# A recurrence and local-attention kernel on one NeuronCore: the first tile of each layer, the first up-projection, the recurrence gates and the split of w1 in other places

## The chip, the core and the metric

The kernel runs on one core of a Trainium2 chip. The core has a matrix engine (TensorE, PE), three elementwise engines (VectorE or DVE, ScalarE or ACT, GpSimd or POOL) and a sync engine (SP) that issues the DMAs. Each engine takes its own instructions strictly in the written order, and they wait for each other through semaphores. The metric is the device time of one execution in microseconds (us).

## What is computed

The input x is 16 sequences of 512 rows with 128 features. After a layer norm (xn) two branches use it, and the output is x + s * silu(f).

```python
def _layernorm(x): m = mean(x, -1); v = var(x, -1); return (x - m) / sqrt(v + 1e-05)

def recurrence(x):                      # s
    x_conv = causal_depthwise_conv(x, conv_w, conv_b)          # width 4
    r_t = sigmoid(x_conv @ W_r.T + b_r); i_t = sigmoid(x_conv @ W_i.T + b_i)
    a_t = sigmoid(log_a) ** (8.0 * r_t)
    h_t = a_t * h_(t-1) + sqrt(clip(1.0 - a_t * a_t, 0.0)) * i_t * x_conv
    out = h @ W_out.T
    return out * rsqrt(mean(out * out) + 1e-06) * gamma

def layer(x):                           # f, applied twice (DEPTH = 2)
    h = shift_token(x)                  # half of the features come from the row before
    q, k, v = split(h @ wqkv)           # 8 heads of 64
    q, k = l2norm(q) * q_scale, l2norm(k) * k_scale
    q, k = rotary_xpos(q, k)
    o = softmax(8 * q @ k.T + mask) @ v # windows of 64 rows, looking at this one and the last
    x = x + o @ wo
    h = layernorm(shift_token(x)) * lg + lb
    a, g = split(h @ w1 + b1)           # 128 -> 2 x 341
    return x + (a * gelu(g)) @ w2 + b2
```

## The kernel before

Everything stays in SBUF: X holds the 16 sequences transposed (features on the partitions), A the copy for the recurrence, B the normalised activations. A sequence has four tiles of 128 rows, so a layer has NT = 64 tiles and NB = 16 sequences. The order on every engine is written out by hand: each engine's function runs the same loops, and what stands in an iteration is chosen by the iteration number.

**Attention of a layer** is `for i in range(NT + 4)`. In iteration i, PE makes q and k of tile i (`qk_proj`, six matmuls into banks 0 and 1), turns q and k of tile i-2 (`turn_qk`, L234 and L237), works out its scores (`sims`), turns the softmax of tile i-3 (`turn_p`, L224), applies tile i-4 to the values (`attend`) and makes v of tile i (`v_proj`). ACT squares q and k (`square`, L530), takes the root (`norm_rt`), the exponentials (`exps`, L556) and copies (`keep_q`, `keep_v`, `keep_p`, `keep_o`). DVE applies the rotary tables (`rotate`, L802 and L793), sums the squares (`norm_sum`, L809), copies k (`keep_k`, L840 and L841) and finds the row maximum (`row_max`, L821). POOL adds (`add_qk`) and scales (`scale_qk`) q and k and normalises the softmax, all through L1040. `qk_proj` of a tile waits until `rotate` has read the tile before it, since both use banks 0 and 1.

Between these stand the other steps, one sequence in four iterations: in layer 0 the input layer norm of a sequence (`ln_stats` on DVE, `ln_root` on ACT, `ln_apply` on POOL L1067, `ln_turn` on PE L172, `ln_keep` on ACT L474, then a DMA that shifts a half into hsh, then `shift_hi` L1076 and `shift_lo` L1040 on POOL, which split it into the two parts hT that the matmuls use); in layer 1 the recurrence (`rec_decay`, `rec_a2`, `rec_root` L725, `rec_root2`, `rec_input`, `rec_scan`, `rec_out`, `rec_gamma`); in both the projection with wo and the second layer norm (`mean`, `centre`, `square_hc`, `var`, `log_var`, `root_var`, `scale_hc`).

**The last four iterations of attention** (i = 64 to 67) drain it. In iteration 66 w1 is scaled and split into w1r (ACT L685, DVE L999) and the first sequence into hnr; at the end of 67 PE makes the bias from w1 (`bias1`).

**The up and down loop** is `for b in range(NB + 3)`: `up(b)` is 18 matmuls with w1r (three chunks j, each a gate part into bank 3+j and an input part into bank j), ACT applies gelu (L603), DVE multiplies (`hidden`, L903), `down` is six matmuls, `down_add` (L909) adds to X. In layer 0 the gates of the recurrence are made here: `conv` on DVE (L725, L918), `gates` and `gates2` on PE and tanh on ACT (L608, L614). `gates(b-1)` and `gates2(b-1)` stand in iteration b, so sequence 15's come in iteration 16, next to `qk_proj(1, 0)`, the first tile of layer 1. Iterations 1 and 2 also finish the layer norm of sequence 15, for which ACT loads the table set with Ln and Exp. In layer 1 the loop holds `end_turn`, `rec_scale`, `end_out` and the stores.

SBUF space is shared in time: w1r and hnr of the up and down loop lie over t1, t2, t3 and sqk of attention, and hxf over P, PT, qT and a part of kT.

## Time and profile before

| | before |
|---|---|
| median of 3 runs | 1361.43 us (1360.09 to 1361.75) |
| the profiled execution: its own time | 1365.7 us |
| its span, first to last instruction | 1363.9 us |
| mean granted TensorE clock | 0.987 |
| busy: PE, DVE, ACT, POOL | 1273.0, 1112.1, 1109.0, 1019.8 us |

From the trace, the stages are: the start until about 46 us; attention of layer 0 until 556.8; its up and down loop until about 699; attention of layer 1 until 1236.9; its up and down loop and the output until the end. Busy PE time counts matmuls whose ends are modelled, and a matmul at the lower clock level counts for twice as long. So a stage is read by three things together: PE's busy time, its granted clock, and what its idle time waited for.

### The profile page before, as it was taken

The page shows a single profiled execution, that of the slowest core. Times are in us where ns is not written, and L with a number is a line of the kernel's source. Part 1 is how long each engine was busy: PE and PEld are TensorE (multiplying, and loading weights), DVE is VectorE, ACT ScalarE, POOL GpSimd, SP SyncE. Part 2 cuts the span into 40 slices and gives each one's busy share as a digit, 9 for nine tenths or more (in the row PEclk, how much of TensorE's full clock was granted, in tenths as well). Part 3 has the DMA queues.
Part 4 walks back from the last instruction along what each step waited for, and adds up shares of the span by engine and source line. Part 5 has one row for each costly group of instructions (what it writes and reads, how often), then busy time and mean ns, then how long its engine had stood idle before and what let it go on. Part 6 is the DMA issues. An engine that isn't in the chain of part 4 may idle for free.

```text
span 1363.9 us, 37604 instructions
## 1 busy us (share of the span) xinstructions
PE 1273.0 (93%) x13656; PEld 994.9 (73%) x13656; DVE 1112.1 (82%) x1929; ACT 1109.0 (81%) x3418; POOL 1019.8 (75%) x712
## 2 busy tenths in 40 slices
PE   2799999999999999899978999999999999999997
PEld 1687887878788787555547788888878888876664
DVE  3788888888888886578768898999889999873887
ACT  2689999999998998564448999999999999997664
POOL 4799999999999987212138999999999999972110
PEclk9899999999999999999989999999999999999999
DMA  5222222222222211011011212211122112110222
GB/s 154 51 60 60 67 60 60 67 60 60 60 73 65 65 41 33 16 32 29 0 26 33 47 45 47 50 44 44 46 55 48 44 44 48 37 32 25 77 72 83
DMA packets 60599, 70.33 MB, mean 52 GB/s; under 512 B 8960, under 2 KB 38528, under 8 KB 60416
## 3 DMA queue, kind: packets, MB, share of 16 engines
q1 hardware_dynamic: 60416, 67.93, 20.0%
q8 instruction: 110, 1.80, 0.6%
q14 instruction: 73, 0.60, 0.1%
HBM read 13.40 MB, written 4.19 MB: 13 GB/s over the span
## 4 chain that ended last, share of the span: by engine, by line
PE 85%; ACT 5%; issue 4%; DVE 3%; POOL 1%; SPq 1%; DMA 1%; ACTq 0%; DVEq 0%
PE ps L167 68%; PE ps L224 9%; PE ps L234 4%; PE ps L237 4%; ACT P L556 2%; DVE t L793 1%; POOL side L1067 0%; PE ps L172 0%; DMA B<-in_k_scale 0%; PE ps L377 0%; ACT qT L577 0%; DVE nm L821 0%; DVE t L802 0%; ACT sqk L530 0%; ACT Vn L570 0%
## 5 line engine op out<-in xcount | busy, mean ns | idle before, releaser
L556 ACT ACTIVATE P<-ps,nm 128x128 f32<-128x128 f32 x1024 | 364.4, 385 | 5.2 <-DVE nm L821 5.2
L167 PE MATMUL ps<-wqkv,hT 128*128 128x512 f32 x1152 | 332.2, 432 | 28.0 <-DVE t L793 12.3
L1040 POOL TENSOR_TENSOR P<-P,rden 128x512 f32<-128x512 f32 x256 | 293.0, 1151 | 42.8 <-DVE rden L828 40.7
L1040 POOL TENSOR_TENSOR t<-t 128x1024 f32<-128x1024 f32 x128 | 306.5, 2395 | 19.1 <-DVE t L793 17.3
L167 PEld LDWEIGHTS ps<-wqkv,hT 128*128 128x128 f32 x1152 | 218.4, 192 | 106.1 <-issue 39.4
L1040 POOL TENSOR_TENSOR t<-t,rr 128x1024 f32<-128x1024 f32 x128 | 243.6, 1903 | 26.1 <-ACT rr L539 25.9
L556 ACT ACTIVATION_READ_ACCUMULATOR P<-ps,nm 128x1 f32 x1024 | 231.1, 226 | 0.0
L802 DVE TENSOR_TENSOR t<-ps,tabl 128x512 f32<-128x512 f32 x256 | 164.2, 683 | 48.1 <-ACT sqk L530 46.9
L546 ACT ACTIVATE PT<-ps 128x1024 f32<-128x1024 f32 x128 | 130.6, 1020 | 75.0 <-PE ps L224 74.0
L1040 POOL TENSOR_TENSOR hnr<-B,hnr 128x512 fp32r<-128x512 f32 x32 | 41.2, 1287 | 198.7 <-ACT hnr L594 198.7
L821 DVE TENSOR_REDUCE nm<-ps 128x4 f32<-128x512 f32 x256 | 173.8, 680 | 6.8 <-PE ps L167 6.8
L793 DVE TENSOR_TENSOR t<-ps,tabl 128x1024 f32<-128x1024 f32 x128 | 155.3, 1213 | 0.0
L809 DVE TENSOR_REDUCE sums<-sqk 128x16 f32<-128x1024 f32 x128 | 154.6, 1208 | 0.0
L530 ACT ACTIVATE sqk<-ps 128x1024 f32<-128x1024 f32 x128 | 137.9, 1077 | 13.7 <-PE ps L167 9.8
L167 PE MATMUL ps<-hnr,w1r 128*128 128x512 f32 (+1 forms) x576 | 146.2, 407 | 0.5 <-DVE hxf L903 0.3
L224 PE MATMUL ps<-idf,P 128*128 128x128 f32 x1024 | 142.2, 281 | 2.1 <-POOL P L1040 2.0
L841 DVE COPY kT<-ps 128x512 f32<-128x512 f32 x128 | 87.9, 686 | 62.7 <-PE ps L237 62.4
L167 PE MATMUL ps<-kT,qT 64*64 64x128 f32 x4096 | 136.3, 271 | 0.0
L167 PE MATMUL ps<-PT,Vs 128*64 128x64 f32 x2048 | 133.2, 229 | 0.4 <-ACT Vn L570 0.2
L167 PEld LDWEIGHTS ps<-kT,qT 64*64 64x64 f32 x4096 | 123.7, 134 | 8.4 <-issue 0.3
L224 PEld LDWEIGHTS ps<-idf,P 128*128 128x128 f32 x1024 | 109.1, 140 | 26.8 <-issue 22.9
L167 PEld LDWEIGHTS ps<-hnr,w1r 128*128 128x128 f32 (+1 forms) x576 | 100.2, 176 | 37.0 <-issue 7.6
(120 smaller groups left out, 2445.6 us busy)
## 6 DMA issues: line engine op xcount, KB each, us to landing
Vs<-Vn SPq DMA_DIRECT2D x224, 128.0 KB, 2.3
side<-in_x SPq DMA_DIRECT2D x16, 256.0 KB, 3.2
hsh<-X SPq DMA_DIRECT2D x32, 128.0 KB, 2.3
A<-X SPq DMA_DIRECT2D x16, 256.0 KB, 2.5
h<-X SPq DMA_DIRECT2D x32, 128.0 KB, 2.3
oT<-in_x SPq DMA_DIRECT2D x16, 256.0 KB, 3.0
out<-oT SPq DMA_DIRECT2D x16, 256.0 KB, 2.4
hsh<-X SPq DMA_DIRECT2D x32, 127.8 KB, 2.3
```

The costliest lines, as they stand in the source:

```text
L167: return e.matmul(o, lhsT, rhs, start=start, stop=stop, skip_group_check=True)
L224: k = e.transpose(ps[:, 5 + g // 4, (g % 4) * 128:(g % 4 + 1) * 128], P[:, g, :], idf[:])
L234: k = e.transpose(ps[:, 5, c * 128:(c + 1) * 128], c0[:, c * 128:(c + 1) * 128], idf[:])
L530: act(heads(sqk[:]), ps[:, 0:2, :].rearrange("p i (h e) -> p (i h) e", e=DH), ACT.Square).then_inc(s_sq, 1)
L546: act(PT[:], ps[:, 5:7, :].rearrange("p s (g q) -> p (s g) q", g=4), ACT.Copy).then_inc(s_PT, 1)
L556: k = act(P[:, g, :], ps[:, 3 + s, (g % 4) * 128:(g % 4 + 1) * 128], ACT.Exp, bias=nm[:, g:g + 1], accum_out=den[:, g:g + 1])
L793: e.tensor_tensor(o1, qk, C, ALU.mult).then_inc(s_t2, 1)
L802: e.tensor_tensor(o2[:, :, :, 32 * s:32 * s + 32], qk[:, :, :, 32 - 32 * s:64 - 32 * s], S[:, :, 32 * s:32 * s + 32].unsqueeze(2).to_broad ...
L809: e.tensor_reduce(sums[:, :, 0], heads(sqk[:]), AX, ALU.add).then_inc(s_ss0, 1)
L821: e.tensor_reduce(nm[:, 4 * s:4 * s + 4], S4, AX, ALU.max, negate=True).then_inc(s_nm, 1)
L841: e.tensor_copy(kT[:, :, s0:s0 + 128], ps[:, 6, :].rearrange("p (c q) -> p c q", c=4)).then_inc(s_kt, 1)
L1040: return e.tensor_tensor(o, a, b_, op)
```

## The change

It has six parts.

1. **The first tile of a layer a cycle ahead.** `turn_qk`, `sims`, `keep_q`, `keep_k` and `row_max` of tile 0 move from iteration 2 to iteration 1, and `norm_rt` of tile 0 from iteration 1 to 0. In layer 1, `rotate` and `norm_sum` of tile 0 and its `qk_proj` and `square` move into iteration b = 15 of layer 0's up and down loop. The zeroing of kT and Vs becomes `no_tile`: in layer 0 the first thing on POOL, in layer 1 in iteration 1, with `rec_a2(0)` and `rec_a2(1)` behind it.
2. **The first up-projection in the drain of attention.** `up(0)` is taken apart into `up_in` and `up_gate`: two input parts ahead of `turn_p` in iteration 66, two gate parts behind it, the third gate part in iteration 67, the third input part in the loop.
3. **w1 at home.** w1r has space of its own, w1 is loaded into the space of sq and rsd, and `bias1` and the two steps of the split move to iterations 2, 3 and 4 of a layer. The space of t1 and t2 is no longer shared with the up and down loop (`kept`).
4. **Gates shifted by a sequence.** `gates(b)` and `gates2(b)` stand in iteration b, and `conv(b + 1)` one iteration ahead of `hidden(b + 1)`; `conv(0)` is in the drain.
5. **The input layer norm's last step** on POOL is x * rst + nmr in place of (x - mean) * rst, with nmr = -mean * rst made by two more instructions per sequence, and `ln_apply(1)` stands behind the first `shift_hi` and `shift_lo`. wqkv's third part is split ahead of the tables.
6. **Smaller ones.** One preloaded table set in iteration 2 of the loop where Ln and Exp each brought a load; one `rec_rms` in place of two; `rec_root` as a tensor_tensor with min; `set_decay` in iterations 9 to 11.

The diff, cut:

```diff
+            sp_("kept", [128, 2048])
             hnr = sp_("hnr", [128, 2, 2, L], F32R)
...
+            def up_gate(l, b, j):
+                m, (o, n) = l * NB + b, CH[j]
+                if b:
+                    e.wait_ge(s_gl, 3 * (m - 1) + j + 1)
+                elif j < 2:
+                    e.wait_ge(s_e, 2 * (l + 1) * NT - 1 + j)
+                else:
+                    e.wait_ge(s_PT, (l + 1) * NT)
+                three(l, b, 3 + j, HID + o, n).then_inc(s_ug, 1)
+
+            def up_in(l, b, j):
+                m, (o, n) = l * NB + b, CH[j]
+                if b:
+                    e.wait_ge(s_hxf, 3 * (m - 1) + j + 1)
+                elif j == 0:
+                    e.wait_ge(s_wlo, 4 * (l + 1))
+                    e.wait_ge(s_hnlo, m + 1)
+                    e.wait_ge(s_t2, (l + 1) * NT)
+                elif j == 2:
+                    e.wait_ge(s_xadd, 2 * (l + 1) * NB)
+                three(l, b, j, o, n).then_inc(s_ua, 1)
...
-                    if 0 <= i - 2 < NT:
+                    if 0 < i - 2 < NT:
                         turn_qk(l, i - 2)
...
+                    if i == NT + 2:
+                        up_in(l, 0, 0)
+                        up_in(l, 0, 1)
                     if 0 <= i - 3 < NT:
                         turn_p(l, i - 3)
+                    if i == NT + 2:
+                        up_gate(l, 0, 0)
+                        up_gate(l, 0, 1)
+                    if i == NT + 3:
+                        up_gate(l, 0, 2)
+                    if i == 2:
+                        bias1(l)
...
+                        turn_qk(l, 0)
+                        sims(l, 0)
                 for b in range(NB + 3):
-                    if b < NB:
+                    if 0 < b < NB:
                         up(l, b)
-                    if l == 0 and b == NB:
-                        e.wait_ge(s_hxf, 3 * NB)
+                    if l == 0 and b < NB:
+                        gates(b)
+                    if b == 0:
+                        up_in(l, 0, 2)
+                    if l == 0 and b == NB - 1:
+                        e.wait_ge(s_hxf, 3 * NB - 1)
                         qk_proj(1, 0)
...
+                    if i == 0:
+                        norm_rt(l, 0)
...
+                    if i == 1:
+                        keep_q(l, 0)
+                    if i == 3:
...
+                        act(w1r[:, 0, :], w1, ACT.Copy, scale=lcol(l, 0)).then_inc(s_whi, 1)
+                    if i == NT + 1:
+                        e.wait_ge(s_tpk, (l + 1) * NT)
+                        split_hn(l, 0)
...
                     if b == 2:
+                        e.preload_act_table_set(ATTN)
                         log_var(l, NB - 1, 7)
                         root_var(l, NB - 1)
-                        if l:
-                            rec_rms(1)
...
+                        if l == 0 and b == NB - 1:
+                            for p in range(3):
+                                rotate(1, 0, p)
+                            norm_sum(1, 0)
+                        if l == 0 and b + 1 < NB:
+                            conv(b + 1)
...
                 e.wait_ge(s_ln, b + 1)
+                tt(nmr[:], mv[:, :, 0], rst[:], ALU.mult).then_inc(s_nmr, 1)
+                e.wait_ge(s_nmr, 2 * b + 1)
+                e.tensor_scalar(nmr[:], nmr[:], -1.0, None, ALU.mult).then_inc(s_nmr, 1)
+                e.wait_ge(s_nmr, 2 * b + 2)
                 if b:
                     e.wait_ge(s_tx, b)
                 for t in range(TPB):
-                    k = e.tensor_scalar(xnb[:, t * 128:(t + 1) * 128], xb[:, t, :], mv[:, t, 0:1], rst[:, t:t + 1],
-                                        ALU.subtract, ALU.mult)
+                    k = e.tensor_scalar(xnb[:, t * 128:(t + 1) * 128], xb[:, t, :], rst[:, t:t + 1], nmr[:, t:t + 1],
+                                        ALU.mult, ALU.add)
...
-            ln_apply(0)
-            ln_apply(1)
...
             for l in range(DEPTH):
                 if l == 0:
+                    no_tile()
+                    ln_apply(0)
                     shift_hi(0, 0)
                     shift_lo(0, 0)
+                    ln_apply(1)
```

On POOL, at the very start, this stood before (layer norm of sequences 0 and 1, the zeroing, then hT of sequence 0):

```order
L1067 TENSOR_SCALAR side<-side,mv,rst 128x128 [waits s_ln]
L1067 TENSOR_SCALAR side<-side,mv,rst 128x128 x3
L1067 TENSOR_SCALAR side<-side,mv,rst 128x128 [waits s_tx,s_ln]
L1067 TENSOR_SCALAR side<-side,mv,rst 128x128 x3
L1107 MEMSET kT 128x4x64
L1108 MEMSET Vs 64x512
L1076 TENSOR_SCALAR hT<-hsh 128x512 [waits s_hsh]
L1040 TENSOR_TENSOR hT<-hsh,hT 128x512 [waits s_hi]
```

And this stands there now:

```order
L1138 MEMSET kT 128x4x64
L1139 MEMSET Vs 64x512
L1070 ISA
L1070 TENSOR_TENSOR nmr<-mv,rst 128x4 [waits s_ln]
L1096 TENSOR_SCALAR nmr<-nmr 128x4 [waits s_nmr]
L1101 TENSOR_SCALAR side<-side,rst,nmr 128x128 [waits s_nmr]
L1101 TENSOR_SCALAR side<-side,rst,nmr 128x128 x3
L1110 TENSOR_SCALAR hT<-hsh 128x512 [waits s_hsh]
L1070 TENSOR_TENSOR hT<-hsh,hT 128x512 [waits s_hi]
L1070 TENSOR_TENSOR nmr<-mv,rst 128x4 [waits s_ln]
```

The split of sequence 0 has moved ahead of the norm of sequence 1, and each norm has two small new instructions in front.

On PE, in iterations 66 and 67 of layer 0, the softmax of tile 63 is turned (L224), and then, before, everything else of the drain, the bias (cols,w) and `up(0)` (hnr,w1r) follow:

```order
L224 MATMUL ps<-idf,P 128x128 [waits s_pn,s_kt,s_qk]
L224 MATMUL ps<-idf,P 128x128 x3
L224 MATMUL ps<-idf,P 128x128 [waits s_pn]
L224 MATMUL ps<-idf,P 128x128 x3
L167 MATMUL ps<-rsd,avg 128x512 [waits s_sqh,s_xadd]
L167 MATMUL ps<-PT,Vs 64x64 [waits s_vlo3,s_o,s_vhi3,s_PT]
...
L167 MATMUL ps<-oT,wo 128x256 [waits s_o,s_rv]
L167 MATMUL ps<-oT,wo 128x256 x3
L167 MATMUL ps<-cols,w 128x1 [waits s_t2,s_w1]
...
L167 MATMUL ps<-hnr,w1r 128x512 [waits s_e,s_hnlo,s_wlo]
```

Now, at the same place (side,wr is `gates`):

```order
L172 MATMUL ps<-hnr,w1r 128x512 [waits s_t2,s_hnlo,s_wlo]
L172 MATMUL ps<-hnr,w1r 128x512 x5
L231 MATMUL ps<-idf,P 128x128 [waits s_pn,s_kt,s_qk]
...
L172 MATMUL ps<-hnr,w1r 128x512 [waits s_e]
L172 MATMUL ps<-hnr,w1r 128x512 x2
L172 MATMUL ps<-norm,avg 128x512 [waits s_sqh,s_xadd]
L172 MATMUL ps<-PT,Vs 64x64 [waits s_vlo3,s_o,s_vhi3,s_PT]
...
L172 MATMUL ps<-hnr,w1r 85x512 [waits s_PT]
L172 MATMUL ps<-hnr,w1r 85x512 x2
L172 MATMUL ps<-oT,wo 128x256 [waits s_o,s_rv]
```

Fifteen of the 18 matmuls of `up(0)` have moved to places ahead of the last projection (oT,wo), and the bias is gone from here.

On DVE, at the passage from layer 0 to layer 1, stood before (from the last `hidden`'s iteration on: L909 is `down_add`, L922 `gates2`, L725 with s_a2 `rec_root`):

```order
L909 SCALAR_TENSOR_TENSOR X<-ps,cols,X 128x512 [waits s_y]
L922 SCALAR_TENSOR_TENSOR A<-oT 128x512 [waits s_ti]
L802 TENSOR_TENSOR t<-ps,tabl 128x16x32 [waits s_add,s_tabm,s_sq,s_ua]
L802 TENSOR_TENSOR t<-ps,tabl 128x16x32
L793 TENSOR_TENSOR t<-ps,tabl 128x1024 [waits s_tpk]
L909 SCALAR_TENSOR_TENSOR X<-ps,cols,X 128x512 [waits s_y]
L922 SCALAR_TENSOR_TENSOR A<-oT,side 128x512 [waits s_ti]
L725 TENSOR_SCALAR side<-side 128x512 [waits s_a2]
L809 TENSOR_REDUCE sums<-sqk 128x16 [waits s_sq]
L813 TENSOR_REDUCE ss<-sums 128x16 [waits s_rr0,s_ss0]
L802 TENSOR_TENSOR t<-ps,tabl 128x16x32 [waits s_add,s_sq]
```

And now:

```order
L826 TENSOR_TENSOR t<-ps,tabl 128x16x32 [waits s_tabm,s_add,s_sq]
L826 TENSOR_TENSOR t<-ps,tabl 128x16x32
L817 TENSOR_TENSOR t<-ps,tabl 128x1024 [waits s_tpk]
L833 TENSOR_REDUCE sums<-sqk 128x16 [waits s_sq]
L837 TENSOR_REDUCE ss<-sums 128x16 [waits s_rr0,s_ss0]
L933 SCALAR_TENSOR_TENSOR X<-ps,cols,X 128x512 [waits s_y]
L946 SCALAR_TENSOR_TENSOR A<-oT 128x512 [waits s_ti]
L933 SCALAR_TENSOR_TENSOR X<-ps,cols,X 128x512 [waits s_y]
L865 COPY kT<-ps 128x4x128 [waits s_sim,s_zero,s_tpk]
L826 TENSOR_TENSOR t<-ps,tabl 128x16x32 [waits s_add,s_sq]
```

The rotation and the sums of tile 0 have moved ahead of both of the last two `down_add`, `rec_root` has gone behind tile 1, and the copy of k of tile 0 has come ahead of the rotation of tile 1.

## Rows read from the trace of the kernel before

**Rows 1.** Page: share of the chain that ended last, by engine.

```profile
PE 85%; ACT 5%; issue 4%; DVE 3%; POOL 1%; SPq 1%; DMA 1%; ACTq 0%; DVEq 0%
```

**Rows 2.** Stretches: span, busy PE, PEld, DVE, ACT, POOL, granted clock, DMA.

```profile
68.00:102.00 34.00, 32.98 (x411) 27.67 (x410) 29.39 (x57) 29.80 (x103) 32.64 (x24) 1.00 0.24 60
...
602.00:636.00 34.00, 34.00 (x114) 20.32 (x113) 27.88 (x42) 15.99 (x26) 5.17 (x4) 1.00 0.20 54
```

**Rows 3.** Stretches of 2 us, same columns: drain of layer 0, start of layer 1.

```profile
548.00:550.00 2.00, 1.32 (x9) 0.86 (x8) 0.00 (x0) 0.93 (x3) 1.04 (x1) 0.97 0.00 0
550.00:552.00 2.00, 2.00 (x18) 0.87 (x18) 0.00 (x0) 2.00 (x4) 0.53 (x1) 0.50 0.03 8
...
706.00:708.00 2.00, 0.00 (x0) 0.00 (x0) 1.84 (x3) 0.03 (x1) 1.42 (x2) 0.72 0.00 0
708.00:710.00 2.00, 0.00 (x0) 0.00 (x0) 0.98 (x2) 1.97 (x4) 0.42 (x1) 0.50 0.01 4
```

**Rows 4.** Timeline of the start: start us, us, engine, line, operation, idle before it.

```profile
0.24 0.10 POOL L1337 MEMSET const-float32-0.0<- 128x1 f32 x1 [0.24 <-issue]
...
10.61 0.60 ACT L474 ACTIVATE X<-ps 128x512 f32<-128x512 f32 x1 [3.38 <-PE ps L172]
...
15.11 3.12 POOL L1067 TENSOR_SCALAR side<-side,mv,rst 128x128 f32<-128x128 f32 x4 [5.76 <-ACT rst L470]
...
18.91 0.61 POOL L1076 TENSOR_SCALAR hT<-hsh 128x512 fp32r<-128x512 f32 x1
...
21.01 2.90 PE L167 MATMUL ps<-wqkv,hT 128*128 128x512 f32 x6 [10.44 <-POOL hT L1040]
...
26.51 0.60 SPq L1167 DMA_DIRECT2D hsh<-X  x1
...
28.07 4.41 PE L167 MATMUL ps<-wqkv,hT 128*128 128x512 f32 x12 [3.51 <-DVE wqkv L772]
...
35.35 2.92 PE L167 MATMUL ps<-wqkv,hT 128*128 128x512 f32 x6 [2.87 <-DVE t L793]
```

**Rows 5.** Waits between 100 and 500 us: total us, times, longest.

```profile
PEld ps L234 <- POOL t L1040: 2.4, 12, 0.2
```

**Rows 6.** POOL's and DVE's lines in a steady stretch of layer 0, and L1067 in all.

```profile
311.81 1.29 DVE L840 COPY kT<-kT 128x256 f32<-128x256 f32 x1 [0.75 <-PE ps L237]
...
L1067 POOL TENSOR_SCALAR side<-side,mv,rst x64: 787/795/1397, 5.6 to 466.3; 128x128 f32<-128x128 f32 x64
```

**Rows 7.** Timeline of the drain of layer 0 and the first iterations of its loop.

```profile
549.10 0.66 PE L224 MATMUL ps<-idf,P 128*128 128x128 f32 x4 [0.68 <-POOL P L1040]
...
553.89 1.96 PE L167 MATMUL ps<-oT,wo 128*128 128x256 f32 x8 [0.79 <-ACT oT L586]
555.70 1.25 PE L167 MATMUL ps<-cols,w 128*128 128x1 f32 x12
...
557.29 1.28 ACT L603 ACT_TABLE_LOAD   x1 [2.50 <-DVE b1g L872]
...
571.95 4.77 PE L167 MATMUL ps<-hnr,w1r 128*128 128x512 f32 x18
...
591.34 1.12 PE L167 MATMUL ps<-oT,wr 128*128 128x512 f32 x2 [0.78 <-ACT B L608]
```

**Rows 8.** Timeline from the last down-projection of layer 0 into layer 1.

```profile
697.14 1.02 ACT L530 ACTIVATE sqk<-ps 128x1024 f32<-128x1024 f32 x1
...
703.96 2.56 DVE L725 TENSOR_SCALAR side<-side 128x512 f32<-128x512 f32 x1 [2.04 <-POOL side L1040]
...
711.50 2.93 PE L167 MATMUL ps<-wqkv,hT 128*128 128x512 f32 x6 [6.49 <-DVE t L793]
...
721.22 1.67 PE L167 MATMUL ps<-wqkv,hT 128*128 128x512 f32 x6 [0.42 <-DVE t L793]
```

**Rows 9.** Timeline of the end of the drain of layer 1.

```profile
1229.79 0.66 PE L224 MATMUL ps<-idf,P 128*128 128x128 f32 x4 [0.17 <-POOL P L1040]
...
1236.90 3.30 PE L167 MATMUL ps<-hnr,w1r 128*128 128x512 f32 x13
```

224 lines of the change are left out of this document (102 added, 122 removed).

## The prediction

> **What bounds the kernel now.** I read first the chain that ended last: 85% of the span is PE's [rows 1]. Then the stretches: in attention PE is busy for 32.98 of 34 us and POOL for 32.64, in the up and down loop PE for 34.00 of 34, all at the full clock level (granted 1.00, 2.4 GHz) [rows 2]. So in the long middle of each stage no reordering of other engines' work can give much, and the time to be had lies at the seams: the start, the two drains of attention, the passage from layer 0 to layer 1. There PE idles, and behind the idling the granted clock falls to 0.50, the 1.2 GHz level: in the drain of layer 0 PE was busy for 1.32 of 2 us when the clock began to fall, and in the passage it fell while PE had nothing to do at all [rows 3]. Last I read, in the timelines, which wait ends last at each seam.
>
> **Part by part.** The sums are made against the span of 1363.9 us. The profiled execution took 1365.7 us, 4.3 above the median of 1361.43; what I subtract from the span I subtract from the median.
>
> *The start.* Before, hT of sequence 0 was ready for splitting from about 14.2 us (the copy to X ended at 11.2, and the DMA needs about 3 us with its issue), but the split stood behind `ln_apply(1)`, 3.12 us from 15.11 on, and began at 18.91. The first `qk_proj` began at 21.01; the second stood behind `v_proj(0)`, which waited 3.51 us for the third part of wqkv, and the third began at 35.35 [rows 4]. The new order takes both waits away: the split at about 12.5 (if `ln_apply(0)` is done some 2 us earlier; 14.5 if not), `qk_proj(0)` 2.1 us later at 14.6, 6.4 ahead of 21.01. But most of this is given back. `turn_qk(0)` now stands ahead of `qk_proj(2)`, and it needs `scale_qk(0)`, which on POOL stands behind the split of sequence 1. That needs `ln_keep(1)` on ACT, which now waits behind `norm_rt(0)`: square and rotation and sum of tile 0 (1.0 + 2.4 + 1.4 us after the 2.9 of `qk_proj`) end at 22.3, so the copy ends at 23.5 against 25.98, its second DMA is issued near 24.1 against 26.51 [rows 4], and split and scaling (1.9 + 1.9 us after a landing of 2.3) give `turn_qk(0)` at 30.4. Turning at the low clock takes 1.7, then DVE copies k (0.7), does the statistics of sequence 2 (1.3) and the rotation (2.4): `qk_proj(2)` at 36.6, later than 35.35. Tile 0's scores are then already done, so the next cycle is shorter: `qk_proj(3)` at about 43.3 against 45.06. I take **1.7 us**, and 1.3 more because the third `ln_apply`, which in this cycle stands alone in front of `scale_qk(2)`, is shorter: **3.0**. Bounds: -2 (the split at 14.5 and a dearer norm) and 6.4 (nothing given back).
>
> *The norm on POOL, 16 times.* Four instructions over 128x128 took 795 ns each in the median; `shift_hi`, a multiply and an add with constants over four times as many columns, took 0.61 in one [rows 4, 6]. The new form is the same pair of operations, with two columns as operands, for which the trace has no row. Lower bound 0.15 (a quarter of 0.61), upper bound the longest of the old form, 1.40 [rows 6]. I take 0.25, since the nearest row in operations is `shift_hi`. The two 128x4 instructions have no row either; I take 0.55 with their two waits, between 0.2 (twice the 0.10 of the memset of one column that opens the trace [rows 4]) and 1.6 (two at the old form's 0.79). That makes 4 x 0.25 + 0.55 = 1.55 for 3.12. What of it reaches PE: in the steady stretch `turn_qk` waited for POOL 12 times in 400 us, 2.4 us in all, once per sequence [rows 5], so 0.2 x 15 = **3.0**. Another piece may come where DVE's kT copy (1.29 us for 128x256 [rows 6]) ran until POOL's instruction beside it ended; I count nothing for it, and 7 as the upper bound, 0.5 a sequence. If the form is no cheaper, 4 x 0.79 + 0.55 = 3.7 is 0.55 more per sequence, and 8 are lost in place of 3 gained.
>
> The Trainium skill ("GPSIMD Engine Reference", section "Engine selection") says that on GpSimd one-input work runs at roughly line rate and two-input work at half. The old form, one input and 795 ns for 128 columns, does not agree with that; `shift_hi`'s row does. By that rule the new form would cost about what I take, and the sum would stay.
>
> *The drain of layer 0.* From the end of `attend(62)` (546.7) PE waits twice for POOL's softmax (1.1 and 0.68), for the copy (then 8 us of which 3.4 at half clock), and 0.79 for oT; then the bias, 1.25, and `up(0)` from 556.81 [rows 7]. A part j is three matmuls, 0.8 us (4.77 / 18 x 3). Laid out anew at the full clock: two input parts to 548.3, `turn_p(63)` to 549.7 (its second half is still bound by 549.10), two gate parts to 551.2, `var` to 551.7, `attend(63)` to 552.8, the third gate part to 553.6, the projection to 555.2. Then ACT is late next: root, split and a table load of 1.28 us, three gelus and tanh end at 558.7, and `gates2(0)`, which stands ahead of `up(1)`, waits for it. `up(1)` from 559.6, `gates(1)`, `down(0)`, `gates2(1)`, `mean`, and `up(2)` at 569.9 against 571.95 [rows 7]: **2.0 us**, with one sequence's gates more behind it, which counts in the passage. Bounds 0 and 5.3 (the 4.0 of the 15 moved matmuls and the 1.25 of the bias).
>
> *Iteration 2 of the loops.* One table load of 1.28 us fewer in layer 0, two in layer 1. In layer 0 PE waited 0.78 us for ACT behind them [rows 7], in layer 1 less. **0.8** together; 0 to 2.
>
> *The passage.* Let T be the end of `up(15)`, 689.8. Before, `gates(15)`, `down(15)`, `gates2(15)` followed `qk_proj(1,0)`; its square was at 697.14, `rec_root(0)` held DVE for 2.56 us in front of the sums, and `qk_proj(1,2)` began at 711.50 = T + 21.7, `qk_proj(1,3)` at 721.22 = T + 31.4 [rows 8]. Now: gates (0.9), `qk_proj(1,0)` (1.6), `down(14)` (2.6), `gates2(15)` (0.9) to T + 5.9; DVE rotates and sums to T + 7.5 and only then does `down_add(14)`, for which `down(15)` waits until T + 8.2: a new wait of 2.3 us on PE. `v_proj(0)`, `qk_proj(1)`, `v_proj(1)` to T + 14.0, `turn_qk(0)` to 14.9, the copy of k to 15.7, and only behind it the rotation of tile 1 to 18.2: `qk_proj(1,2)` there, 3.5 ahead. Square 1.0, sums, two `rec_root` at 0.7 (from a tensor_tensor of 0.68), rotation 2.4: `qk_proj(1,3)` at T + 24.6, 6.8 ahead. POOL then binds one cycle and takes 0.8 back: 6.0. PE still idles for 2.3, 1.2 and 2.7 us of these 25, and before, less idling than that brought the clock down in the drain [rows 3], so I take off 1.5 for some work at the low level: **4.5**. Bounds 1 (the low level through the whole fill) and 7.
>
> *The drain of layer 1.* The same layout with less idling: `turn_p(63)`'s second half at 1229.79, `up(0)` at 1236.90 [rows 9]. New: PE is full from 1229.0 to the projection's end at 1237.1, ACT then needs root, `rec_rms`, split, load and gelu to 1239.2, and `up(1)` starts there against 1241.6 (1236.9 + 4.77): **2.4**; 0 to 5.
>
> *What is moved elsewhere.* Bias (1.25 on PE), scaling of w1 (0.85 on ACT), its rest (1.35 on DVE) now stand in iterations 2 to 4 of each layer. There PE waits for other engines, so the bias hides; the 1.35 on DVE may lengthen a cycle by half: **-0.7** each, **-1.4** in all. w1's second load stands behind `shift_h` and a wait for s_hn on SP's queue; only `load_w2(1)` is behind it, which waits anyway until the end of the loop. `conv(b+1)` comes no earlier before its use than `conv(b)` did; `set_decay` is 2 us of tiny steps under PE. The later `rec_root` at 0.68 for 0.53 hides. Zero for all of them.
>
> Sum: 3.0 + 3.0 + 2.0 + 0.8 + 4.5 + 2.4 - 1.4 = 14.3. Span 1349.6; time 1361.4 - 14.3 = 1347.1, say **1347**.
>
> **Rivals.** (a) *The new form of the norm is not cheaper on POOL.* Against it speaks `shift_hi`; for it, that no row has columns as operands at that price. Then the steady term is -8 for +3, and the start about 0 for 3: 14.3 - 11 - 3 = 0.3 to 3 better at the full price, about 5 if half the price comes through: 1356 to 1361, taken as 1357. (b) *The seams stay bound by their chains.* The new waits named above (`ln_keep(1)` behind `norm_rt(0)`, `down_add(14)` behind the rotation, the copy of k ahead of tile 1's rotation) and the low clock level eat the gain, each term at its lower third: about 6 better, 1355. (c) *Slower.* The four-instruction norm at its dearest row, 1.40 us each, costs 4 x 1.40 + 0.55 = 6.15 per sequence, 3 more than now, right in front of `scale_qk`, for which PE already waits there; 15 x 3 = 45 less a slack of about 1 each, 30, minus the 8 of the seams: 1383. It decides from 0.75 us per sequence on, where 15 x 0.75 equals the 11.3 that the other terms give, that is at 0.83 us per instruction (3.12 + 0.75 - 0.55, over 4), hardly above the old 0.795. (d) *The steady stretch of layer 0 gives the kT copies too*: 7 more, 1340.
>
> The Trainium skill ("SBUF — State Buffer", section "Who interferes with whom") says that a VectorE copy in a two-port mode and a GpSimd instruction exclude each other for their whole length, whoever comes first. The 1.29 us copy agrees with it; by that rule a shorter norm shifts which instruction the copy meets, and does not take the meeting away, which is why (d) is not the forecast.
>
> **How the numbers follow.** Forecast 0.56 (1342 to 1352), (a) 0.14, (b) 0.14, (c) 0.07, (d) 0.09. A measurement of this kernel can tell about 0.2%, 2.7 us, from no change: 1358.7 to 1364.1. A third of (a) and a fifth of (b) fall in it: same 0.08; slower is (c) with a little of (a): 0.08; faster 0.84. The range leaves out (c) and the ends of (a), (b) and (d): 1340 to 1358.
>
> **What would show it.** Right: `qk_proj(0,0)` near 14.6 and `qk_proj(0,3)` near 43; the norm's line on POOL at about 0.25 us and no wait of `turn_qk` for POOL per sequence; 15 matmuls of `up(0)` ahead of the last projection and `up(2)` of layer 0 about 2 us earlier relative to `attend(62)`; `down(15)` waiting some 2 us for `down_add(14)`; `qk_proj(1,3)` 25 to 27 us after `up(15)`. Wrong: POOL's norm instructions above 0.8 us, a longer interval between equal tiles in attention of layer 0, or a clock of 0.50 for as long as before at the passage.

## The result and the profile after

| | before | changed |
|---|---|---|
| median | 1361.34 us (1360.09 to 1361.75, 4 runs) | 1353.37 us (1352.94 to 1354.10, 4 runs) |
| the profiled execution: its own time, its span | 1365.7, 1363.9 us | 1352.9, 1351.1 us |
| ratio, 95% interval | | 0.9944 (0.9926 to 0.9961) |

The change makes the kernel 8.0 us faster by the medians of this set, which is 0.6%. In a later set of runs the kernel before came out at 1367.69 us and the changed one at 1353.60: ratio 0.9899 (0.9885 to 0.9912), 14.1 us. The changed kernel repeats, the kernel before does not (1361.3, 1365.7, 1367.7 and 1363.3 us in four sets).

Where the time went is read best from one event that occurs once per tile in both kernels: the start of `turn_qk` on PE. Between its starts at chosen tiles, and from the last of them to `down`, lie the stages. Each kernel was profiled twice, and the measured gain is given over all pairings of the two profiles.

| stage (us) | before, twice | changed, twice | forecast gain | measured |
|---|---|---|---|---|
| start to tile 8 of layer 0 | 103.84, 103.48 | 101.95, 102.00 | 2.3 | 1.5 to 1.9 |
| tile 8 to 12 | 32.40, 31.47 | 35.92, 35.97 | 0 | -3.5 to -4.5 |
| tile 12 to 63 | 402.12, 402.10 | 397.18, 397.18 | 3.0 | 4.9 |
| tile 63 to down(1) | 39.06, 39.19 | 37.34, 37.33 | 2.0 | 1.7 to 1.9 |
| down(1) to tile 4 of layer 1 | 169.45, 168.37 | 164.21, 163.84 | 4.5 and part of 0.8 | 4.2 to 5.6 |
| tile 4 to 63 | 473.15, 472.00 | 473.50, 473.62 | -0.7 | -0.3 to -1.6 |
| tile 63 to down(3) | 50.25, 51.22 | 47.39, 47.56 | 2.4 and part of 0.8 | 2.7 to 3.8 |
| down(3) to the end | 93.63, 93.67 | 93.61, 93.70 | 0 | 0 |

The chain that ended last, by engine, has hardly changed (page of the changed kernel; compare [rows 1]), and the long middle of the loop is as full as it was (stretch, columns as in [rows 2]). In the drain of layer 0 the granted clock no longer falls (compare [rows 3]). In the passage it still does, but for two spells of 3.4 us each (from 692.2 and from 709.3), where it had stood at 0.50 for 13.7 us (from 706.9):

```profile
PE 83%; ACT 5%; issue 4%; DVE 3%; DMA 2%; POOL 2%; SPq 1%; ACTq 0%; DVEq 0%; POOLq 0%
```

```profile
602.00:636.00 34.00, 34.00 (x114) 20.30 (x113) 27.16 (x42) 15.41 (x24) 7.58 (x6) 1.00 0.17 46
...
548.00:550.00 2.00, 2.00 (x25) 1.15 (x25) 0.00 (x0) 0.76 (x2) 0.00 (x0) 1.00 0.00 0
550.00:552.00 2.00, 2.00 (x26) 1.43 (x21) 0.00 (x0) 1.60 (x4) 0.00 (x0) 1.00 0.00 0
692.00:694.00 2.00, 2.00 (x4) 0.87 (x3) 0.40 (x1) 1.30 (x2) 1.97 (x1) 0.56 0.00 0
```

The start, timeline of the changed kernel (compare [rows 4]): the first `qk_proj` comes at 15.99 us, where it had come at 21.01. Then `turn_qk(0)` waits until 31.67 for the scaling, which stood behind the split of sequence 1, and the third `qk_proj` comes at 37.92, later than the 35.35 of before:

```profile
15.99 2.90 PE L172 MATMUL ps<-wqkv,hT 128*128 128x512 f32 x6 [5.93 <-POOL hT L1070]
...
24.24 0.58 ACT L500 ACTIVATE X<-ps 128x512 f32<-128x512 f32 x1
...
27.79 0.62 POOL L1110 TENSOR_SCALAR hT<-hsh 128x512 fp32r<-128x512 f32 x1 [2.93 <-DMA hsh<-X]
28.49 1.26 POOL L1070 TENSOR_TENSOR hT<-hsh,hT 128x512 fp32r<-128x512 f32 x1
29.71 1.90 POOL L1070 TENSOR_TENSOR t<-t,rr 128x1024 f32<-128x1024 f32 x1
31.67 1.12 PE L241 MATMUL ps<-idf,t 128*128 128x128 f32 x4 [4.67 <-POOL t L1070]
...
37.92 2.93 PE L172 MATMUL ps<-wqkv,hT 128*128 128x512 f32 x6 [1.10 <-DVE t L817]
```

In this stretch the granted clock stands at 0.50 for some 22 us (from 24 to 46), where before it stood there from 28 to 30 and from 36 to 44.

The norm's line on POOL, and the carried copy of kT on DVE (L840 before, L864 now) between 140 and 520 us, first of the changed kernel, then of the kernel before (compare [rows 6]; columns of the groups: total us, mean ns, idle before it). One instruction of the norm takes 452 ns in place of 795, and with it the copy became shorter, 976 ns in the mean for 1585, though it was not changed:

```profile
L1101 POOL TENSOR_SCALAR side<-side,rst,nmr x64: 447/452/1424, 6.1 to 464.0; 128x128 f32<-128x128 f32 x64
...
L864 DVE COPY kT<-kT 128x256 f32<-128x256 f32 x12 | 11.7, 976 | 9.1 <-PE ps L244 9.1
```

```profile
L840 DVE COPY kT<-kT 128x256 f32<-128x256 f32 x12 | 19.0, 1585 | 9.0 <-PE ps L237 9.0
```

The wait of [rows 5], `turn_qk` for POOL, 12 times, is gone from the changed kernel's list for 137 to 535 us but for one. In the same list PE's idle time that ended in no wait the profile shows ("issue") fell with the copy, and PE now waits for a DMA three times (first of the changed kernel, then of the kernel before):

```profile
PE ps L172 <- issue: 4.3, 6, 0.8
...
PE ps L172 <- DMA norm<-X: 1.7, 3, 0.7
```

```profile
PE ps L167 <- issue: 10.1, 12, 1.5
```

New ahead of that stretch, in tile 8's cycle, is ScalarE's wait for the constants of the decay (`set_decay`). Timeline of the changed kernel:

```profile
100.68 2.38 POOL L1070 TENSOR_TENSOR t<-t 128x1024 f32<-128x1024 f32 x1
...
101.90 0.15 DVE L752 TENSOR_SCALAR ab<-ab 128x1 f32<-128x1 f32 x1
...
101.97 1.10 DVE L760 TENSOR_TENSOR ab<-cols,ab 128x1 f32<-128x1 f32 x1
...
103.11 0.20 ACT L712 ACTIVATE ab<-ab 128x1 f32<-128x1 f32 x1 [2.35 <-DVE ab L760]
```

The passage (compare [rows 8]; `gates(15)` begins at 683.45) and the drain of layer 1 (compare [rows 9]):

```profile
691.48 4.54 PE L172 MATMUL ps<-hxf,w 128*128 128x512 f32 x6 [2.19 <-DVE X L933]
...
702.79 1.66 PE L172 MATMUL ps<-wqkv,hT 128*128 128x512 f32 x6 [1.00 <-DVE t L817]
...
708.87 2.58 PE L172 MATMUL ps<-wqkv,hT 128*128 128x512 f32 x6 [2.51 <-DVE t L817]
```

```profile
1225.60 1.97 PE L172 MATMUL ps<-oT,wo 128*128 128x256 f32 x8
1228.09 0.91 PE L172 MATMUL ps<-hnr,w1r 128*85 128x512 f32 x3 [0.52 <-DVE X L873]
```

The drain of layer 0 has a new wait too. `conv(0)`, which part 4 of the change put there, holds VectorE for 3.5 us in front of the copy of k of tile 63, and the scores of tile 63 wait 1.77 us for that copy. They start 3.94 us behind `turn_qk(63)`; before, they waited 1.02 us for ScalarE and started 3.19 us behind it. First the changed kernel, then the one before:

```profile
534.04 1.23 DVE L749 TENSOR_SCALAR side<-A,cols 128x512 f32<-128x512 f32 x1
535.31 2.32 DVE L942 SCALAR_TENSOR_TENSOR side<-A,cols,side 128x511 f32<-128x511 f32 x3
...
538.21 0.69 DVE L865 COPY kT<-ps 128x512 f32<-128x512 f32 x1
...
538.99 0.41 PE L172 MATMUL ps<-mask,idb 64*64 64x512 bf16 x4 [1.77 <-DVE kT L865]
```

```profile
541.55 0.41 PE L167 MATMUL ps<-mask,idb 64*64 64x512 bf16 x4 [1.02 <-ACT qT L577]
```

### The profile page after: what moved, and what is told of

Its sections match the earlier page's. It is cut to its first block, busy times and chain, and to the rows that moved or that the text cites. A ratio compares the mean times of both kernels' runs of the same rounds, so it can differ in the third digit from the quotient of the medians.

```text
span 1351.1 us, 37630 instructions
## 1 busy us (share of the span) xinstructions
PE 1274.2 (94%) x13656; PEld 996.8 (74%) x13656; DVE 1104.1 (82%) x1929; ACT 1105.8 (82%) x3413; POOL 1009.0 (75%) x744
## 4 chain that ended last, share of the span: by engine, by line
PE 83%; ACT 5%; issue 4%; DVE 3%; DMA 2%; POOL 2%; SPq 1%; ACTq 0%; DVEq 0%; POOLq 0%
PE ps L172 66%; PE ps L231 9%; PE ps L241 4%; PE ps L244 4%; ACT P L580 2%; DMA norm<-X 1%; DVE t L817 1%; POOL t L1070 1%; DVE t L826 1%; ACT Vn L594 0%; PE ps L391 0%; PE ps L177 0%; DMA hsh<-X 0%; DVE sums L833 0%; POOL side L1101 0%
## 5 line engine op out<-in xcount | busy, mean ns | idle before, releaser
L1070 POOL TENSOR_TENSOR P<-P,rden 128x512 f32<-128x512 f32 x256 | 296.9, 1166 | 48.4 <-DVE rden L852 45.9
L1070 POOL TENSOR_TENSOR t<-t,rr 128x1024 f32<-128x1024 f32 x128 | 243.8, 1905 | 16.6 <-ACT rr L563 16.5
```

The lines of the kernel that those rows point to most:

```text
L1070: return e.tensor_tensor(o, a, b_, op)
```

## The experiments

Ratios are to the kernel before, which ran beside each set: at 1365.66 us in the first (decay_spread, old_norm, new_norm_before, start_order), 1367.69 in the second (after_again, copy_psum, drain_back, best1), 1363.31 in the third (decay_in_before, before_again, bias_weight, best2). The changed kernel itself ran in the second set only; a difference to it from another set leans on its two medians, 1353.37 and 1353.60. "Tiles 12 to 63" means the interval of `turn_qk` in layer 0.

One profile of a stage carries scatter. Kernels whose code is the changed kernel's up to the drain of layer 0 reached tile 8 at 101.95 and 102.00 (the changed kernel, twice), 103.01 (bias_weight) and 103.50 us (drain_back), and took 397.2, 397.2, 394.5 and 399.0 us from tile 12 to 63. So a difference of 1.5 us at the start, or of 2 to 4 us between tiles 12 and 63, shows nothing by itself.

### What the constants of the decay cost

**decay_spread**, changed kernel:

```diff
-                    if l == 0 and i == 9:
+                    if l == 0 and i == 10:
-                    if l == 0 and i == 10:
+                    if l == 0 and i == 12:
-                    if l == 0 and 9 <= i < 12:
-                        set_decay(i - 9)
+                    if l == 0 and i in (9, 11, 13):
+                        set_decay((i - 9) // 2)
```

> The changed kernel with one edit: the two steps of the decay's constants on ScalarE stand in iterations 10 and 12, and VectorE's three parts in 9, 11 and 13, so that ScalarE finds each input ready. Theory (the constants cost three cycles): in the changed kernel turn_qk of tiles 8 and 12 of layer 0 stand at 101.95 and 137.87 us, 35.92 apart, where the kernel before had 103.84 and 136.24, 32.40 apart; ScalarE waited 2.35 and 0.90 us for VectorE's ab there. Without these waits the interval from tile 8 to tile 16 comes back to within 0.7 of the 63.97 of the kernel before (67.71 now), and the time falls by about 3.3 us to 1350.1. Rival 1 (VectorE's tiny steps with two inputs, 1.10 and 1.58 us long, are the cost): they are still there, the interval falls by under 1.2 us and the time stays above 1352. Rival 2 (another cause, such as the phase between the norm and the tiles): no change, 1353.4.

Measured: 1350.89 us (1348.96 to 1351.96), ratio 0.9885 (0.9867 to 0.9902). Tiles 8 to 16 took 65.13 us, between the 67.71 of the changed kernel and the 63.96 before: 2.6 of 3.7 came back, 1.2 stayed. ScalarE no longer waited for ab, so its wait was the larger part. VectorE's steps of one column with two inputs still took 1.10 us (L760), 1.14 and 1.35 us; that the 1.2 left over is theirs was not tested apart.

**decay_in_before**, kernel before, the other way round:

```diff
-                    if l == 0 and i < 3:
-                        set_decay(i)
+                    if l == 0 and 9 <= i < 12:
+                        set_decay(i - 9)
```

and ScalarE's two steps in 9 and 10 in place of 0 and 1.

> The kernel before with one edit: the constants of the decay are made in iterations 9 to 11, as in the changed kernel, and not in 0 to 2. Theory (this move alone costs the changed kernel 3.5 us): turn_qk of tile 8 to that of tile 12 of layer 0 takes 35.5 to 36.5 us in place of 32.40 (the changed kernel: 35.92 and 35.97), ScalarE waits 2 to 2.5 us for ab once; the start gains 0 to 1; the time rises by 2.5 to 4 us against the kernel before of the same set. Rival (only together with the changed kernel's other timing): the interval stays under 33.5 and the time within 1 us.

Measured: 1366.81 us (1365.97 to 1369.15), ratio 1.0030 (1.0017 to 1.0044), 3.5 us slower than the kernel before beside it. Tile 8 to 12 took 36.77 us, for 32.40 and 31.47 in the two profiles of the kernel before; ScalarE waited 2.31 and 0.90 us. So the move alone costs there what the changed kernel loses there, and more: 4.4 to 5.3 us, of which the start, rid of these steps, gave 1.3 to 1.7 back (tile 8 at 102.19 for 103.84 and 103.48). The trace shows why: POOL's instruction runs from 100.87 to 103.26, and VectorE's step of one column ends with it.

```profile
100.87 2.39 POOL L1040 TENSOR_TENSOR t<-t 128x1024 f32<-128x1024 f32 x1
102.26 1.01 DVE L736 TENSOR_TENSOR ab<-cols,ab 128x1 f32<-128x1 f32 x1
103.31 0.20 ACT L677 ACTIVATE ab<-ab 128x1 f32<-128x1 f32 x1 [2.31 <-DVE ab L736]
```

### The norm's form

**old_norm**, changed kernel (and without the two lines that make nmr):

```diff
-xb[:, t, :], rst[:, t:t + 1], nmr[:, t:t + 1], ALU.mult, ALU.add)
+xb[:, t, :], mv[:, t, 0:1], rst[:, t:t + 1], ALU.subtract, ALU.mult)
```

> The changed kernel with the norm on GpSimd as it was: four times (x - mean) * rst, without the two instructions for nmr. Theory (the norm's form alone makes the steady stretch of layer 0 shorter): turn_qk of tile 12 to that of tile 63 takes 397.18 us in the changed kernel and took 402.12 before; with the old form it takes 401.5 to 402.5, and with 0.5 to 1 us more at the start the time rises by 5 to 6 us to 1358.5 to 1359.5. Rival (the gain there came from the first tile being a cycle ahead, so from another phase between the engines): the interval stays below 399, the time at 1353.5 to 1355.

**new_norm_before**, kernel before with the same lines the other way.

> The kernel before with the norm's new form alone: x * rst + nmr in four instructions, nmr in two more. Theory (as above, the form alone): the interval of turn_qk from tile 12 to tile 63 falls from 402.12 to about 397.2, the start gains 0.5 to 1 us, time 1355.5 to 1356.5. Rival (another phase): interval over 400.5, time 1359.5 to 1361.5.

Measured: old_norm 1365.91 us (1363.05 to 1368.42), ratio 1.0004 (0.9993 to 1.0015), tiles 12 to 63 in 407.12 us, not the 402 expected. new_norm_before 1355.20 us (1354.14 to 1357.25), ratio 0.9923 (0.9910 to 0.9937), 397.62 us, as expected. So the form alone, of all that was changed, brings the kernel before 10 us, and without it the changed kernel gains nothing. At the start the form alone gave the kernel before 3.4 to 3.7 us (tile 8 at 100.11), more than the whole change gave (101.95), and without it the changed kernel reached tile 8 at 103.80, no earlier than the kernel before. Old_norm's interval was 5 us longer than either theory said, its time over 6 us longer, and that led to the copy of kT: in old_norm 10 of the 11 copies between 150 and 490 us take 2.27 to 2.29 us, in the kernel before 5 of the 12 between 120 and 480. Why it is so many more there stays open. The copies of old_norm between 140 and 520 us:

```profile
L864 DVE COPY kT<-kT 128x256 f32<-128x256 f32 x12 | 25.0, 2084 | 9.2 <-PE ps L244 9.2
```

The timeline of the kernel before shows the long form of it. POOL's instruction ends at 344.43; VectorE's copy has waited since 343.30, but POOL's next one, whose input is ready, goes first, and the copy ends when that does:

```profile
342.06 2.37 POOL L1040 TENSOR_TENSOR t<-t 128x1024 f32<-128x1024 f32 x1
...
343.30 2.27 DVE L840 COPY kT<-kT 128x256 f32<-128x256 f32 x1 [0.76 <-PE ps L237]
344.38 1.05 POOL L1040 TENSOR_TENSOR P<-P,rden 128x512 f32<-128x512 f32 x1
```

In the short form (311.81, 1.29 us [rows 6]) the copy ends with POOL's first instruction, and POOL's next follows it. The new norm lets POOL reach this place earlier, so the copy meets less of that instruction: 0.52 or 1.53 us in the changed kernel. A sequence of layer 0 takes 31.5 us before with a short copy and 32.4 with a long one; now it takes 30.8 with a short copy and 31.65 with a long one. Behind a short copy a second wait shows in the changed kernel: the `mean` of the second layer norm waits up to 0.7 us for the DMA that brings it X shifted by a row (norm<-X, three times in the list above), and those sequences take 31.4 to 31.7 us as well. Timeline of the changed kernel, from a sequence whose copy took 0.52 us:

```profile
252.76 1.10 PE L172 MATMUL ps<-norm,avg 128*128 128x512 f32 x2 [0.61 <-DMA norm<-X]
```

These two, the long copies and this DMA, account for the scatter of tiles 12 to 63: 3 long copies of 11 and 1.0 us of DMA wait in bias_weight (394.5), 9 of 11 and 0.5 us in drain_back (399.0).

 The Trainium skill ("SBUF — State Buffer", section "Who interferes with whom") says that a VectorE copy in a two-port mode and a GpSimd instruction keep each other out for a whole instruction, and that the order of issue decides who is blocked. The trace agrees as to the lock (1.29 and 2.27 us for one copy). As to the order it adds a case: the copy at 343.30 had been waiting for over 1 us when POOL's instruction of 344.38 came, and still came after it.

**before_again**, the kernel before, unedited:

> The kernel before, unedited, for a second profile. Its time came out as 1361.3, 1365.7 and 1367.7 us in three sets, the changed kernel's as 1353.4 and 1353.6. Theory (the copy of kT has two durations, 1.29 and 2.27 us, as GpSimd's next instruction lets it pass or not, and a sequence takes 31.5 or 32.35 us with it): in the first profile, of 1365.7 us, 5 of 12 copies were long; in a run of 1367 us some 6 to 8 of 12 are, at other sequences than before, and the rest of the milestones repeat within 0.5 us. Rival (the sets differ by something else, such as the start or layer 1): the number of long copies is the same and the difference sits elsewhere.

Measured: 1363.64 us (1362.36 to 1367.57), profiled at 1363.25. 5 of 12 copies were long, as in the first profile, but three of them in other sequences; tiles 12 to 63 took 402.10 us. So the places change from run to run and the number did not; the 2.4 us between the two profiles sit at the start (0.4), in tile 8 to 12 (0.9), in the passage (1.1) and in layer 1 (1.2, with 1.0 given back in its drain). The rival has it. Why the sets of the kernel before differ by up to 6 us stays open; the three sets ran on three different chips, and no run tells the chip from other causes. **after_again**, the changed kernel, unedited:

> The changed kernel once more, unedited, beside the others of this set, so that their times have a common base: the kernel before took 1365.66 us in the last set and 1361.34 earlier. Expected: a ratio of 0.991 to 0.996 to the kernel before. Its profile tells which of the discrete values of a sequence's period in layer 0 (about 30.85 or 31.65 us, with a copy of kT of 0.52 or 1.53 us) repeat at the same sequences (a fixed cause) and which change places (a race between VectorE and GpSimd).

Measured: 1353.60 us (1352.67 to 1354.71), ratio 0.9899 (0.9885 to 0.9912). Short and long copies changed places here too; every stage repeats within 0.4 us.

**copy_psum**, changed kernel:

```diff
-                if t == 2:
-                    e.wait_ge(s_kt, n)
-                    e.tensor_copy(kT[:, :, 0:64], kT[:, :, 256:320])
+                if t == 1:
+                    e.tensor_copy(kT[:, :, 0:64], ps[:, 6, :].rearrange("p (c q) -> p c q", c=4)[:, :, 64:128])
```

> The changed kernel with one edit: the carried 64 columns of kT, which a VectorE copy from kT to kT brought in every fourth tile, are copied from PSUM one tile earlier. Theory (that copy, held while GpSimd's instruction runs, is what the norm's form changed): in 12 sequences of layer 0 the copy took 1585 ns in the mean before, 976 now, 2084 in the changed kernel with the old norm and 1054 in the kernel before with the new norm, and PE's idle time there went with it, 10.1, 4.3, 16.1 and 5.0 us. The new copy takes about 0.4 us, as the addition of 128x256 from PSUM does (0.39 to 0.42), and waits for nobody; the intervals of a sequence in layer 0 lie within 0.3 of each other, tile 12 to 63 takes 391 to 395 us in place of 397.2; in layer 1, where PE idles 0.8 us per sequence beside a copy of 1.15 us, the period falls from 32.30 to 31.5 to 31.9. Time 8 to 15 us under the changed kernel. Rival 1 (the copy only hides another wait that is as long: the scores wait for the whole cycle of GpSimd): periods unchanged within 0.2, time within 2 us of the changed kernel. Rival 2 (VectorE now lacks the time in the cycle of tile 1): the gain of one cycle is lost in another.

Measured: 1352.13 us (1351.42 to 1353.34), ratio 0.9889 (0.9875 to 0.9902). The copy itself was as cheap as expected (424 ns, never held), but in layer 0 the long wait went to VectorE's next instruction with all operands in SBUF, `scale_hc` (B<-norm), 2139 ns for 730 in after_again; sequences took 31.0 or 32.0 us, and tiles 12 to 63 took 400.9 us, 3.7 more, not the 391 to 395 expected. In layer 1, where no such instruction stands in that cycle, the usual period fell from 32.3 to 31.7, and tiles 4 to 63 took 469.15 us for 473.50. So rival 2 has layer 0 and the theory layer 1, and the whole is 1.5 us under after_again beside it, not 8 to 15. First of copy_psum, then of after_again:

```profile
L886 DVE TENSOR_TENSOR B<-norm 128x512 f32<-128x512 f32 x12 | 25.7, 2139 | 0.0
L863 DVE COPY kT<-ps 128x256 f32<-128x256 f32 x12 | 5.1, 424 | 11.2 <-PE ps L244 11.2
```

```profile
L887 DVE TENSOR_TENSOR B<-norm 128x512 f32<-128x512 f32 x12 | 8.8, 730 | 0.0
```

### The start

**start_order**, changed kernel, on GpSimd:

```diff
-                        if (b := hit(i, -3)) is not None:
+                        if (b := hit(i, -3)) is not None and b > 1:
                             shift_hi(l, b)
                             shift_lo(l, b)
...
                         add_qk(l, i)
+                    if l == 0 and i == 1:
+                        shift_hi(0, 1)
+                        shift_lo(0, 1)
```

> The changed kernel with one edit: on GpSimd the split of sequence 1 (shift_hi, shift_lo) stands behind scale_qk(0) and add_qk(1), not ahead of scale_qk(0). Theory (the early start is given back because turn_qk(0) waits for this split): scale_qk(0) starts at about 24.4 instead of 29.71 us, turn_qk(0) at 26.4 instead of 31.67, qk_proj(2) near 33 instead of 37.92, and from the tile 3 on the kernel is 3 to 5 us earlier than the changed one: turn_qk(8) of layer 0 at 97 to 99 in place of 101.95, time 1348.5 to 1350.5. Rival 1 (the next chain, copy of k, statistics of sequence 2 and rotation on VectorE, or the 1.2 GHz level, takes the time back): turn_qk(0) is early but turn_qk(8) gains less than 1.5 us, time over 1352. Rival 2 (the split comes too late for tile 4): a new wait of qk_proj(4) for hT.

Measured: 1347.34 us (1346.92 to 1349.38), ratio 0.9866 (0.9851 to 0.9881), some 6 us under the changed kernel, of which 4.5 are there by tile 8. Scaling at 24.77, `turn_qk(0)` at 26.73, the third `qk_proj` at 32.10, tile 8 at 97.46 us for 101.95; tile 4's `qk_proj` waited for no split. The granted clock is 1.00 from 26 to 30, where it had been 0.50; it then stands at 0.50 from 31 to 41 us, when PE had idled from 30 to 32.

```profile
24.77 1.90 POOL L1070 TENSOR_TENSOR t<-t,rr 128x1024 f32<-128x1024 f32 x1
26.73 0.42 PEld L241 LDWEIGHTS ps<-idf,t 128*128 128x128 f32 x4 [1.01 <-POOL t L1070]
...
28.00:30.00 2.00, 1.28 (x36) 1.02 (x36) 1.97 (x10) 0.51 (x2) 0.00 (x0) 1.00 0.31 74
```

### The drains

**drain_back**, changed kernel: the calls of `up_in` and `up_gate` in iterations 66 and 67 and behind `gates(0)` are taken out, and

```diff
-                    if 0 < b < NB:
+                    if b < NB:
                         up(l, b)
```

> The changed kernel with the first up-projection back in the loop: all 18 matmuls of up(0) in a row behind the last projection, the rest unchanged. Theory (the moved matmuls fill PE's idle time in the drain and keep its clock up): from turn_qk(63) to up(2) of layer 0 the changed kernel took 531.90 less 0 us, from 535.05 to 566.95, that is 31.90, and the kernel before 33.59; put back, the bias being gone still, it takes 33.0 to 34.5, with a spell at 0.50 of the clock; in layer 1 from turn_qk(63), 1210.10, to up(2), 1236.58, it took 26.48 and takes 28 to 29. Time 3 to 5 us above the changed kernel. Rival (ScalarE's root, split, table load and gelu end last either way): both intervals within 0.7 of the changed kernel's, time within 1.5 us.

Measured: 1356.14 us (1352.99 to 1358.49), ratio 0.9914 (0.9900 to 0.9929), 2.5 us above the changed kernel beside it, a little under the 3 to 5 expected. Layer 0: tile 63 to `up(2)` in 35.2 us for 31.9, with the clock at 0.66 and 0.50 as before the change. That is more than the 33.0 to 34.5 expected and more than the 33.6 of the kernel before; `conv(0)` and the gates of one sequence more now stand ahead of `up(2)`. Layer 1: 26.5 us, as with the moved matmuls; the expectation of 28 to 29 was wrong. There PE waited only 0.52, 0.17, 0.22 and 0.79 us at a time, so the moved matmuls found little to fill: the last projection came 13.3 us after tile 63 with `up(0)` put back and 15.5 with part of it in front.

```profile
550.00:552.00 2.00, 1.81 (x6) 0.85 (x6) 0.00 (x0) 1.02 (x1) 0.13 (x1) 0.66 0.00 0
552.00:554.00 2.00, 2.00 (x29) 1.46 (x30) 0.00 (x0) 0.69 (x1) 0.00 (x0) 0.50 0.00 0
```

**bias_weight**, drain_back with, in iteration 67, 12 matmuls of one column as in `bias1`, which nothing reads.

> The changed kernel with the whole of up(0) back in the loop, as in the run before, and with 12 matmuls of one column more in iteration 67, of the same shape as those of the bias, into an unused part of a bank; nothing reads them. Theory (in layer 1 the drain's gain of 1.9 us is the bias that went away, not the up-projection that was moved, since putting that back cost nothing there): from turn_qk(63) to down(1) of layer 1 the kernel before took 32.94 us, the changed one 31.07 and 31.24, with up(0) put back 31.11; with the extra matmuls 32.2 to 32.6. In layer 0 the same distance to down(0), 30.26 with up(0) put back, rises to 31.3 to 31.8. Rival (ScalarE's chain ends last there, and the gain came from the split of w1 leaving ScalarE): 31.0 to 31.4 in layer 1, no change.

Measured: 1355.14 us (1353.46 to 1356.87), ratio 0.9940 (0.9924 to 0.9955). Layer 1: tile 63 to `down(1)` in 32.64 us, with 31.11 in drain_back and 32.94 and 33.86 before. So of the drain's 1.7 to 2.8 us in layer 1 the bias is 1.5, and the up-projection nothing; the rest is as large as the difference between the two profiles of the kernel before. Layer 0: 30.16 for 30.26 to `down(0)`, where 31.3 to 31.8 was expected. There the last projection stood 15.2 us behind tile 63 and in drain_back 16.5, because in this profile the clock stayed at 1.00 in the drain: the spell at 0.50 cost drain_back as much as the bias costs here. So the spell of 3.4 us at 0.50 cost this drain 1.3 us, and with the up-projection put back `up(2)` comes 3.2 to 3.3 us later, be it with the spell or with the bias. The drain of layer 0 in this profile (compare the rows of drain_back), and the row of layer 1 that answers to the 1.25 us of [rows 7]:

```profile
547.00:549.00 2.00, 1.21 (x33) 1.09 (x30) 0.00 (x0) 1.33 (x4) 0.00 (x0) 1.00 0.00 0
549.00:551.00 2.00, 2.00 (x14) 1.80 (x12) 0.28 (x1) 1.90 (x3) 1.26 (x1) 1.00 0.00 0
```

```profile
1226.97 1.25 PE L172 MATMUL ps<-cols,w1r 128*128 128x1 f32 x12
```

### Put together

**best1** has start_order, copy_psum and two more edits:

```diff
             ln_root(1)
+            e.wait_ge(s_dcy, 1)
+            act(ez, ax, ACT.Exp, scale=-1.0).then_inc(s_ez, 1)
+            e.wait_ge(s_dcy, 2)
+            act(lnu, u, ACT.Ln).then_inc(s_lnu, 1)
             square(0, 0)
...
             ln_stats(1)
+            for part in range(3):
+                set_decay(part)
...
                         down_add(l, b - 1)
+                    if l == 0 and b == NB - 1:
+                        norm_sum(1, 0)
```

> The changed kernel with four edits together: the split of sequence 1 behind scale_qk(0) and add_qk(1), which alone brought the time to 0.9866 of the kernel before; the constants of the decay made at the very start, behind the statistics of sequence 1, where ScalarE and VectorE wait; in the passage down_add(14) ahead of norm_sum(1, 0); and the copy of kT from PSUM. Theory (the terms add up): 6 us for the start, 3.5 for the constants (tiles 8 to 16 in 64.0 in place of 67.7), 1.0 to 1.5 for the passage (down(15) begins 1.4 earlier than 8.03 us behind gates(15), and the 1.2 GHz spell is shorter), 8 to 15 for the copy: 18 to 26 us under the changed kernel. Rival (PE becomes the bound, since it is busy for 98% of the steady stretches): the copy's part is under 5 and the whole under 15.

Measured: 1338.94 us (1336.92 to 1340.13), ratio 0.9790 (0.9776 to 0.9803), 14.7 us under the changed kernel beside it: under the 18 to 26 expected and within the rival's "under 15", since the copy brought some 1.5. Tiles 8 to 16 took 63.2 us: at the start, where POOL was running only the short instructions of the norm (0.20 to 0.45 us each), VectorE's steps of one column took 0.15 to 0.24 us. In the passage `down(15)` came 4.44 us behind `down(14)` for 5.78, waiting 0.84 us:

```profile
16.11 0.15 DVE L758 TENSOR_TENSOR ab<-cols,ab 128x1 f32<-128x1 f32 x1
...
682.89 2.84 PE L172 MATMUL ps<-hxf,w 128*128 128x512 f32 x6 [0.84 <-DVE X L930]
```

**best2** is best1 with the copy from PSUM in layer 1 only, and in layer 0 `ln_stats(2)` behind `norm_sum(0, 1)`.

> The four edits together of the last set (0.9790 of the kernel before), with two alterations: the carried part of kT is copied from PSUM in layer 1 only, and in layer 0 as in the changed kernel; and the statistics of sequence 2 stand behind the rotation of tile 1 on VectorE. Theory (in layer 0 the copy from PSUM handed the long wait to the next instruction of VectorE with SBUF operands only, scale_hc of 1.45 or 2.46 us, with sequences of 31.0 or 32.0 us against 30.85 or 31.65; in layer 1 it took the period from 32.30 to 31.7): turn_qk of tile 12 to 63 of layer 0 in 395.5 to 398.5 us in place of 399.3, layer 1 as in the last set, qk_proj(2) at about 31.2 in place of 32.30; 1 to 4 us under that version, ratio 0.976 to 0.978. Rival (layer 0's interval is a matter of chance between 395 and 400): ratio 0.978 to 0.980.

Measured: 1334.36 us (1331.65 to 1337.44), ratio 0.9795 (0.9780 to 0.9810). By the ratio, where 0.976 to 0.978 was expected, that is no better than best1, as its rival said, since the kernel before ran at 1363.31 in this set; in us it is 4.6 less than best1 and 19 less than the changed kernel, whose two sets agree within 0.3. The third `qk_proj` came at 31.33, tiles 12 to 63 took 394.8 us, and all 12 copies between 110 and 460 us were short (0.52); four sequences still took 31.55 to 31.84 us, each with a wait of 0.5 to 0.8 us for the DMA norm<-X. The same interval took 394.5 us in bias_weight, without these edits, so it does not show what they did. Whether best2 beats best1 is not settled by this; that both beat the changed kernel is.

## Why the prediction was right, and where it was not

The time, 1353.4 us, lies in the range, 6.4 above the forecast of 1347. Point by point:

- **"What I subtract from the span I subtract from the median"** is the step that made most of the 6.4. The spans differ by 12.8 us (1363.9 to 1351.1), near the 14.3 forecast (by the second profiles, 1361.5 to 1351.2, by 10.3); but the profiled execution of the kernel before lay 4.3 above its median, and the changed kernel's 0.4 below its own. Set beside a median of 1367.7, the same kernel is 14.1 faster. How much is gained depends on the runs of the kernel before that it is set against.
- **`set_decay`, "2 us of tiny steps under PE", zero**, is the term that failed: 3.5 to 4.5 us lost between tiles 8 and 12, less what the start gained by it (1.3 to 1.7 in the kernel before), shown by moving it in both kernels. I had counted how long the steps run when nothing holds them. In the middle of attention the step of one column with two inputs took 1.10 us and ended with POOL's instruction of 2.38 us, and ScalarE waited 2.35 us for it with the exponentials behind it.
- **The norm** was mis-sized twice. An instruction took 0.45 us, not 0.25, and the whole took 2.38 in place of 3.12, where 1.55 was forecast; the two 128x4 instructions with their waits took the 0.6 left over, near the 0.55 forecast. The steady gain was 4.9, not 3.0, and for another reason: 11 of the 12 waits of [rows 5] did go, 2.2 us, but the larger piece was the copy of kT, for which the prediction counted nothing, with 7 as the bound (case d). 19.0 us of copies became 11.7, and PE's idle time that ended in "issue" went from 10.1 to 4.3 us. The bound was right and the value taken was wrong. That the term came near is in part luck: an instruction nearly twice as dear as forecast gave more than forecast, by the path that was left out.
- **The start**: 3.0, less 0.7 for the moved work; 1.5 to 1.9 measured. The mechanism was foreseen, `ln_keep(1)` behind `norm_rt(0)` and the split ahead of the scaling, `turn_qk(0)` at 31.67 for the 30.4 given, `qk_proj(0,3)` at 44.42 for 43.3. The first `qk_proj` came at 15.99 and not 14.6, since `ln_apply(0)` ended 0.5 us earlier and not 2. start_order shows what this order costs: 4.5 us by tile 8. The low clock from 24 to 46 us was in the sum only for the turning of tile 0. And the gain that was measured is hardly the order's: the norm's form alone gave 3.4 to 3.7 there in the kernel before, the removal of `set_decay` 1.3 to 1.7, and with the old norm nothing was left (tile 8 at 103.80). So the order itself gave nothing or cost some us; one profile each, with a scatter of 1.5, says no more.
- **The drain of layer 0**: 2.0 forecast, 1.7 to 1.9 measured, and drain_back shows that the moved matmuls are needed for it: put back, they cost 3.3 us, of which 1.3 is the low clock. `conv(0)`, "no earlier before its use" and put at zero, took 0.75 us of the gain through the copy of k. **The drain of layer 1**: 2.4 forecast, 1.7 to 2.8 measured to `up(2)`, but not by the layout that the prediction worked out; bias_weight shows that 1.5 of it is the bias. Right in size, wrong in cause.
- **The passage**: `down(15)` was to wait 2.3 us for `down_add(14)` and waited 2.19; `qk_proj(1,2)` and `(1,3)` were to come at T + 18.2 and T + 24.6 and came 19.3 and 25.4 after T, 683.45 us. From T to tile 4's `turn_qk` it is 3.9 us less than before, for 4.5 (2.8 to 4.3 over all pairings of the profiles).
- **The range** held because its bounds came from rows, and because errors of both signs met: 3.5 lost with `set_decay`, 1.9 won in the steady stretch. The second is luck, since no term of the sum foresaw it.

## What to carry to other kernels

A small step with two inputs in SBUF was not small on VectorE beside a long instruction of GpSimd: 1.10 us for one column beside 2.38 us, and 0.15 to 0.24 at the start of best1. Put such steps where GpSimd has no long instruction, and not where ScalarE waits for them in order. When an instruction on GpSimd becomes shorter, look at what VectorE does beside it, not only at who waits for GpSimd: here the second effect was larger than the first. When that wait is gone, look for the next: here it was a DMA of 0.4 to 0.8 us. And take a forecast from several executions of the kernel before, since a profile of one may hold scatter that the median does not.

## What was not expected of the hardware

- The two operation pairs differ on GpSimd: subtract and multiply with two columns as operands took 795 ns for 128x128 in the median, multiply and add with two columns 452 ns, and a multiply and add with constants took 0.61 us for 128x512.
- A VectorE copy from SBUF to SBUF that waits behind a GpSimd instruction can be passed by GpSimd's next one: the same 128x256 copy took 0.52, 1.29, 1.53 or 2.27 us in most cycles, and from PSUM 0.42 us; the wait then went to the next VectorE instruction with its operands in SBUF (2139 ns for 730 in the mean).
- One and the same passage from layer 0 to 1, with the same code, took 49.2 to 52.0 us from `down(14)` to tile 4's `turn_qk` in six kernels. The spells at 0.50 of the clock fell at other places in each.
